# Attention over channels on one core: turned keys split by transfers inside SBUF, and the key sums' scale moved from the folded matrix to the queries

## The reference, cut to what matters

```
x = x + _L0_xattn_ref(_layernorm(x, axis=-1), ctx, Wq, Wkv, Wout, b_out, g)

q = einsum('oc,bcn->bon', Wq, x);  k, v = split(einsum('oc,bcn->bon', Wkv, context))
q = softmax(q over the 64 channels of a head) * 64 ** -0.5     # 8 heads of 64
k = softmax(k over the 1024 positions)
ctx = einsum('bhdn,bhen->bhde', k, v)
out = einsum('bhde,bhdn->bhen', ctx, q)
out = Wout @ out + b_out, then normalised over the 128 channels, times g
```

## Times and profile before

| | |
|---|---|
| time, median of 3 runs | 2017.39 us (2016.75 to 2019.11) |
| the profiled execution's own time | 2018.59 us |
| its span, first to last instruction | 2016.8 us |
| PE busy in the span | 1910.8 us (95%) |
| DVE busy | 1430.0 us (71%) |
| ACT busy | 996.2 us (49%) |
| POOL busy | 803.7 us (40%) |
| mean granted TensorE clock | 0.992 of full speed |

### The profile page before, as it was taken

The page is one execution under the profiler, slowest core; times in us unless marked ns, Lnnn a source line. Parts: engine busy times, 40 slices in busy tenths (PEclk is TensorE's granted clock), DMA queues, the critical chain, the costliest instruction groups (busy, mean ns, idle before and its releaser), DMA issues. The chain is left out here.

```text
span 2016.8 us, 29785 instructions
## 1 busy us (share of the span) xinstructions
PE 1910.8 (95%) x10780; PEld 1667.0 (83%) x10780; DVE 1430.0 (71%) x2049; ACT 996.2 (49%) x1207; POOL 803.7 (40%) x456
## 2 busy tenths in 40 slices
PE   4999999999999999999998789999999999999999
PEld 3778787878787878787877679999999999999998
DVE  5999999999999999999996664444444544444443
ACT  3777777777777777777776521111111111111111
POOL 3767676767676767676765000000000000000000
PEclk9999999999999999999999889999999999999999
DMA  3111111111111111111111621111111111111110
GB/s 116 47 67 59 68 56 67 59 67 56 68 60 67 58 66 60 66 58 66 60 35 47 179 93 56 49 53 62 62 62 62 62 62 62 62 57 48 51 42 32
DMA packets 43999, 127.64 MB, mean 63 GB/s; under 512 B 4224, under 2 KB 14080, under 8 KB 43968
## 3 DMA queue, kind: packets, MB, share of 16 engines
q1 hardware_dynamic: 39360, 110.44, 15.6%
q0 software_dynamic: 4608, 16.78, 2.6%
HBM read 93.65 MB, written 33.55 MB: 63 GB/s over the span
## 5 line engine op out<-in xcount | busy, mean ns | idle before, releaser
L281 POOL TENSOR_TENSOR kT_lo<-kT,kT_hi 128x1024 fp32r<-128x1024 f32 x128 | 304.7, 2403 | 0.6 <-ACT kT_hi L323 0.5
L277 POOL TENSOR_TENSOR eq<-eq,q_inv 128x1024 f32<-128x1024 f32 x128 | 242.5, 1905 | 143.8 <-DVE q_inv L487 143.8
L960 POOL TENSOR_TENSOR rstd_c<-var_c,minus_half 128x8 f32<-128x8 f32 x32 | 52.7, 1648 | 549.7 <-DVE var_c L1099 549.7
L52 PE MATMUL ps<-w_ra_hi,xT_hi 128*128 128x384 f32 (+1 forms) x768 | 257.2, 335 | 0.0
L54 PE MATMUL ps<-w_ra_hi,xT_lo 128*128 128x384 f32 (+1 forms) x768 | 251.7, 328 | 0.0
L53 PE MATMUL ps<-w_ra_lo,xT_hi 128*128 128x384 f32 (+1 forms) x768 | 251.4, 327 | 0.0
L982 ACT CAST hT_hi<-ps 128x512 fp32r<-128x512 f32 x64 | 37.7, 589 | 374.8 <-PE ps L1156 374.8
L52 PE MATMUL ps<-w_b_hi,hT_hi 128*128 128x512 f32 x512 | 205.4, 401 | 0.0
L338 ACT ACTIVATE ek<-ps,k_min 128x1024 f32<-128x1024 f32 x128 | 143.0, 1117 | 120.3 <-DVE k_min L491 120.3
L54 PE MATMUL ps<-w_b_hi,hT_lo 128*128 128x512 f32 x512 | 200.8, 392 | 0.0
L53 PE MATMUL ps<-w_b_lo,hT_hi 128*128 128x512 f32 x512 | 200.3, 391 | 0.0
(11 more groups left out here) (142 smaller groups left out, 4675.8 us busy)
## 6 DMA issues: line engine op xcount, KB each, us to landing
x_sb<-in_x SPq DMA_DIRECT2D x64, 512.0 KB, 4.1
ctx_sb<-in_ctx SPq DMA_DIRECT2D x32, 512.0 KB, 3.4
ctx_hi<-in_ctx POOLq DMA_DIRECT2D x32, 512.0 KB, 3.6
attention_out<-o_sb SPq DMA_DIRECT2D x32, 512.0 KB, 2.6
o_sb<-attention_out SPq DMA_DIRECT2D x32, 512.0 KB, 3.9
out<-out_sb SPq DMA_DIRECT2D x32, 512.0 KB, 2.9
x<-in_L_ffn_A SPq DMA_DIRECT2D x2, 512.0 KB, 4.1
o_sb<-in_L_ffn_A SPq DMA_DIRECT2D x2, 512.0 KB, 3.6
```

The source lines that it names most:

```text
L52: pe.matmul(out, stat_hi, mov_hi, start=first, stop=False)
L277: pool.tensor_tensor(v, v, per_row(q_inv[:, i, :], 2 * HEADS, DH), ALU.mult).then_inc(q_normed, 1)
L281: pool.tensor_tensor(kT_lo[:, i % 2, :, :], kT[:, i % 2, :, :], kT_hi[:, i % 2, :, :].bitcast(F32), ALU.subtract).then_inc(kT_lo_ready, 1)
```

## The change

Two things change in `attention`.

First, the key sums. `scale_m` and `m_full` go. The factor 64 ** -0.5 moves into Z's two parts, which are made once. One over the key sums is computed early in the step (`invert_keys`, a reciprocal into a double buffer) and multiplied into the turned queries while they are split: `query_hi` becomes an activation with a per-partition scale, `query_lo` a multiply-and-subtract. M is split straight out of PSUM: two casts of 64 x 512 on ACT and two subtractions of 64 x 512 on DVE, the slot being released by the last of these. ACT takes `folded_hi` ahead of `query_hi` 1. `shift_x` moves from DVE to ACT as two 128 x 1 activations.

Second, the turned keys. ACT still copies each piece from PSUM to `kT`. A transfer started by POOL copies `kT` to `kT_hi` in SBUF and converts on the way. ACT writes the negated, rounded `kT` into `kT_lo`, and a second transfer started by POOL adds `kT` to it. Both transfers count on one semaphore per piece, `kT_moved[i]`, for which PE and the copy of piece i+2 wait.

```diff
-        slot_read = {"K": k_exp, "C": cT_lo_ready, "Q": q_shifted, "KT": kT_copied, "M": m_scaled,
+        slot_read = {"K": k_exp, "C": cT_lo_ready, "Q": q_shifted, "KT": kT_copied, "M": m_lo_ready,
...
             def keys_lo(b, i):
-                pool.wait_ge(kT_hi_ready, 4 * b + i + 1)
-                pool.tensor_tensor(kT_lo[:, i % 2, :, :], kT[:, i % 2, :, :], kT_hi[:, i % 2, :, :].bitcast(F32),
-                                   ALU.subtract).then_inc(kT_lo_ready, 1)
+                pool.wait_ge(kT_copied, 4 * b + i + 1)
+                wait_for(pool, t_part, 4 * b + i - 1)
+                pool.sem_inc(kT_issued, 1)
+                pool.dma_start(kT_hi[:, i % 2, :, :], kT[:, i % 2, :, :]).then_inc(kT_moved[i], 16)
+                pool.wait_ge(kT_neg_ready, 4 * b + i + 1)
+                pool.sem_inc(kT_issued, 1)
+                pool.dma_start(kT_lo[:, i % 2, :, :], kT[:, i % 2, :, :], accum_op=ALU.add).then_inc(kT_moved[i], 16)
...
             def keys_copy(b, i):
                 act.wait_ge(kT_turned, 4 * b + i + 1)
-                wait_for(act, kT_lo_ready, 4 * b + i - 1)
+                if i >= 2:
+                    act.wait_ge(kT_moved[i - 2], 32 * b + 32)
+                else:
+                    wait_for(act, kT_moved[i + 2], 32 * b)
                 act.copy(kT[:, i % 2, :, :], slot(f"KT{i}")).then_inc(kT_copied, 1)
 
-            def keys_hi(b, i):
+            def keys_neg(b, i):
                 act.wait_ge(kT_copied, 4 * b + i + 1)
                 wait_for(act, t_part, 4 * b + i - 1)
-                act.copy(kT_hi[:, i % 2, :, :], kT[:, i % 2, :, :]).then_inc(kT_hi_ready, 1)
+                act.activation(kT_lo[:, i % 2, :, :], kT[:, i % 2, :, :], ACT.Copy, bias=0.0,
+                               scale=-1.0).then_inc(kT_neg_ready, 1)
...
-                act.copy(q_hi[:, j % 2, :], flat(f"QT{j}")).then_inc(q_hi_ready, 1)
+                act.activation(q_hi[:, j % 2, :], flat(f"QT{j}"), ACT.Copy, bias=0.0,
+                               scale=k_inv[:, p, j:j + 1]).then_inc(q_hi_ready, 1)
...
             def folded_hi(b):
-                act.wait_ge(m_scaled, 2 * b + 2)
+                act.wait_ge(m_made, b + 1)
                 wait_for(act, o_part, 4 * b)
-                act.copy(m_hi[:, :, :], m_full[:, :, :]).then_inc(m_hi_ready, 1)
+                for h in range(2):
+                    r = slice(h * DH, (h + 1) * DH)
+                    act.copy(m_hi[r, :, :], folded[r, :, h, :]).then_inc(m_hi_ready, 1)
...
-            def scale_m(b, p):
+            def invert_keys(b, p):
                 dve.wait_ge(k_exp, 4 * b + 4)
-                dve.reciprocal(k_inv[:, :], k_sum[:, p, :]).then_inc(k_inv_ready, 1)
-                dve.wait_ge(k_inv_ready, b + 1)
-                dve.wait_ge(m_made, b + 1)
-                wait_for(dve, m_lo_ready, b)
-                made = flat("M0").rearrange("p (j h c) -> p j h c", j=CH, h=2)
-                for h in range(2):
-                    r = slice(h * DH, (h + 1) * DH)
-                    dve.scalar_tensor_tensor(out=m_full[r, :, :], in0=made[r, :, h, :], scalar=DH ** -0.5,
-                                             in1=per_row(k_inv[r, :], CH, P), op0=ALU.mult,
-                                             op1=ALU.mult).then_inc(m_scaled, 1)
+                wait_for(dve, q_lo_ready, 4 * (b - 1))
+                dve.reciprocal(k_inv[:, p, :], k_sum[:, p, :]).then_inc(k_inv_ready, 1)
...
             def folded_lo(b):
-                dve.wait_ge(m_hi_ready, b + 1)
-                dve.tensor_tensor(m_lo[:, :, :], m_full[:, :, :], m_hi[:, :, :].bitcast(F32),
-                                  ALU.subtract).then_inc(m_lo_ready, 1)
+                for h in range(2):
+                    r = slice(h * DH, (h + 1) * DH)
+                    dve.wait_ge(m_hi_ready, 2 * b + h + 1)
+                    dve.tensor_tensor(m_lo[r, :, :], folded[r, :, h, :], m_hi[r, :, :].bitcast(F32),
+                                      ALU.subtract).then_inc(m_lo_ready, 1)
...
             def add_weighted(b, i):
-                pe.wait_ge(kT_lo_ready, 4 * b + i + 1)
+                pe.wait_ge(kT_moved[i], 32 * b + 32)
```

More of the change, by code:

```diff
@@ L109, in attention @@
         t_lo = sb("t_lo", [P, HD], F32R)
-        m_full = sb("m_full", [P, CH, P])
         m_hi = sb("m_hi", [P, CH, P], F32R)
@@ L114, in attention @@
         k_sum = sb("k_sum", [P, 2, CH])
-        k_inv = sb("k_inv", [P, CH])
+        k_inv = sb("k_inv", [P, 2, CH])
         q_max = sb("q_max", [P, 4, 2 * HEADS])
@@ L122, in attention @@
         rstd = sb("rstd", [P, 1])
+        neg_mean = sb("neg_mean", [P, 1])
         shift = sb("shift", [P, 1])
@@ L150, in attention @@
         q_lo_ready, cT_lo_ready = sem("q_lo_ready"), sem("cT_lo_ready")
[L151 to L154, removed]
+        t_lo_ready, k_inv_ready, m_lo_ready = sem("t_lo_ready"), sem("k_inv_ready"), sem("m_lo_ready")
+        x_stats, x_mean_ready, veps_ready = sem("x_stats"), sem("x_mean_ready"), sem("veps_ready")
         k_exp, q_exp, q_hi_ready = sem("k_exp"), sem("q_exp"), sem("q_hi_ready")
-        kT_copied, kT_hi_ready = sem("kT_copied"), sem("kT_hi_ready")
+        kT_copied, kT_neg_ready = sem("kT_copied"), sem("kT_neg_ready")
         cT_hi_ready, t_hi_ready, m_hi_ready, o_copied = (
             sem("cT_hi_ready"), sem("t_hi_ready"), sem("m_hi_ready"), sem("o_copied"))
+        neg_mean_ready, shift_ready = sem("neg_mean_ready"), sem("shift_ready")
         xn_ready, xn_hi_ready = sem("xn_ready"), sem("xn_hi_ready")
-        kT_lo_ready, q_normed = sem("kT_lo_ready"), sem("q_normed")
+        kT_issued = sem("kT_issued")
+        kT_moved, q_normed = [sem(f"kT_moved{i}") for i in range(CH)], sem("q_normed")
         ctx_hi_loaded = [sem(f"ctx_hi_loaded{i}") for i in range(2)]
@@ L178, in attention @@
         acc_flat = acc.rearrange("p a b -> p (a b)")
+        folded = flat("M0").rearrange("p (j h c) -> p j h c", j=CH, h=2)
         def on(kind, s, edge):
@@ L356, in folded_hi @@
             def folded_hi(b):
-                act.wait_ge(m_scaled, 2 * b + 2)
+                act.wait_ge(m_made, b + 1)
                 wait_for(act, o_part, 4 * b)
-                act.copy(m_hi[:, :, :], m_full[:, :, :]).then_inc(m_hi_ready, 1)
+                for h in range(2):
+                    r = slice(h * DH, (h + 1) * DH)
+                    act.copy(m_hi[r, :, :], folded[r, :, h, :]).then_inc(m_hi_ready, 1)
             def norm_x(b, p):
+                act.wait_ge(x_mean_ready, b + 1)
+                act.activation(neg_mean[:, :], mv[:, 0:1], ACT.Copy, bias=0.0, scale=-1.0).then_inc(neg_mean_ready, 1)
+                act.wait_ge(rstd_ready, b + 1)
+                act.wait_ge(neg_mean_ready, b + 1)
+                act.activation(shift[:, :], rstd[:, :], ACT.Copy, bias=0.0, scale=neg_mean[:, 0:1]).then_inc(shift_ready, 1)
                 act.wait_ge(shift_ready, b + 1)
@@ L381, in step @@
                     act.wait_ge(z_folded, 1)
-                    act.copy(z_hi[:, :], z_sum).then_inc(z_hi_ready, 1)
+                    act.activation(z_hi[:, :], z_sum, ACT.Copy, bias=0.0, scale=DH ** -0.5).then_inc(z_hi_ready, 1)
                 if KT:
                     keys_copy(s - 1, 0)
-                    keys_hi(s - 1, 0)
+                    keys_neg(s - 1, 0)
                     keys_copy(s - 1, 1)
-                    keys_hi(s - 1, 1)
+                    keys_neg(s - 1, 1)
                 if O:
@@ L395, in step @@
                     keys_copy(s - 1, 2)
-                    keys_hi(s - 1, 2)
+                    keys_neg(s - 1, 2)
                     keys_copy(s - 1, 3)
-                    keys_hi(s - 1, 3)
+                    keys_neg(s - 1, 3)
                 if K:
@@ L401, in step @@
                 if QT:
-                    query_hi(s - 1, 0)
+                    query_hi(s - 1, 1 - par, 0)
                 if Q:
@@ L408, in step @@
                     exp_keys(s, par, 2)
-                if QT:
-                    query_hi(s - 1, 1)
                 if M:
                     folded_hi(s - 1)
+                if QT:
+                    query_hi(s - 1, 1 - par, 1)
                 if Q:
@@ L415, in step @@
                 if QT:
-                    query_hi(s - 1, 2)
+                    query_hi(s - 1, 1 - par, 2)
                 if X_:
@@ L420, in step @@
                 if QT:
-                    query_hi(s - 1, 3)
+                    query_hi(s - 1, 1 - par, 3)
                 if K:
@@ L459, in weights, with query_lo @@
                 dve.tensor_tensor(w["bias"][:, :], b_col[:, :], b_mean[:, :], ALU.subtract).then_inc(b_step, 1)
-            def query_lo(b, j):
+            def query_lo(b, p, j):
                 dve.wait_ge(q_hi_ready, 4 * b + j + 1)
-                dve.tensor_tensor(q_lo[:, j % 2, :], flat(f"QT{j}"), q_hi[:, j % 2, :].bitcast(F32),
-                                  ALU.subtract).then_inc(q_lo_ready, 1)
```

(29 more changed lines are left out.)

9 lines of the change are left out of this document (3 added, 6 removed).

## The result

The changed kernel takes 2272.54 us (median of 4 runs, 2269.53 to 2275.02) against 2017.07 beside it: a ratio of 1.126, interval [1.1245, 1.1284]. The profiled execution took 2269.53 us with a span of 2267.9. Slower was forecast, but the forecast was 2111 us, +93 us, and the measured loss is +255. That is outside the forecast's own range (2028 to 2180) and where the rival "the accumulation costs two transfers or more" had put it (2208 to 2290).

The account below looks back on a forecast made before the run. PE was taken to set the pace at 33.64 us a step; the first part brought 32.4, transfer waits of 4.1 made 36.5, which over 32 batches is +93 us on 2018.6, so 2111 us, with its range from 2028 to 2180.

Parts of the forecast that it names:

- the accumulation costs two transfers or more: Rival on the keys' low-part transfers: 2208 us, up to 2290 with the store's collision and slower issue; chance 0.25.
- Lying between, with three passes for two, I take 2.25 and keep both ends: Data time of a 512 KB accumulating transfer: 2.25 us taken, between 1.5 (as a plain one) and 3.0.
- The prediction's own walk: Timing of four transfer pairs through POOL's queue: PE waits 1.4, 1.6 and 1.1 us at weighted 0, 1, 3; 4.1 per step.
- the second wait: PE's wait at weighted 1 for low part 1, seen at t = 13.4 but wanted at 11.8: 1.6 us.
- The 0.5 us before turn queries 2: New PE wait because M's slot is released by the second subtraction: about 0.5 us per step, bounds 0 and 0.8.
- The wait at the step's start: PE's wait for the exponentials of keys 3, some 0.2 us really lost, claimed to go as DVE gets lighter.
- cheap end: Accumulating transfer with 1.5 us of data: waits 0.7, 0.8 and 0, a step of 33.9 us, 2028 us.
- the store's collision: Output store's 1.4 us of data falls into low 0, adding up to that to the first wait: 2250 at the upper end.
- at 5 us or so behind its issue the forecast holds: Sign in the `kT_lo` landing: about 5 us the forecast, under 3.5 for low 0 the fast side, over 7 the dear case.
- the dear case: Accumulating transfers costing two plain ones or more: 2208 us, up to 2290; chance 0.25.
- The transfers are hidden: Rival: data time 1.2 us or less, or pairs overlap; waits 0.5, 0.2, 0, 2002 us, 1981 without waits; chance 0.22.
- The M chain gives nothing: Rival: M's slot released 1.5 us late, the first part's gain gone, +35 us; chance 0.05 with middling transfers (2146).

Follow-up runs that it names:

- high part on ACT: Changed kernel with the keys' high part cast by ACT, leaving POOL only the accumulating transfers: 2143.72 us, ratio 1.061 to the kernel before.
- half-size run: Changed kernel with each accumulating transfer cut to the first half of its bytes (256 KB), the other half's low part left out: 2117.39 us, ratio 1.048.
- waits filled: Changed kernel with throwaway products on TensorE ahead of weighted 0, 1 and 3 (9, 6 and 9): 2257.25 us, ratio 1.118.

## Why the prediction was wrong

The direction and the mechanism held: waits at weighted 0, 1 and 3, none at 2, the strict order on POOL, and the queue on the DMA engines. The size did not. Of the 161 us between 2111 and 2272, about 70 are the dearer accumulation, 20 the first part, 55 the store and the clock, and 17 are open.

- **The step that failed** is "Lying between, with three passes for two, I take 2.25 and keep both ends". An accumulating transfer has 2.8 us of data time (high part on ACT) where a plain one has 1.5. The half-size run shows that it is data time. The prediction's own walk at 3.0 us gave 2208, 97 us more than at 2.25. At 2.8 its waits are 2.0, 2.1 and 2.2, and it lies at about 2180. The issues were not the reason: an accumulating one lasts 0.87 us instead of 0.62, but in a row they start 0.57 to 0.59 apart.
- **The store and the clock.** The store was worked out at up to 1.4 us, used for the upper end only and left out of the sum. It cost 1.3 us. The fall of TensorE's clock behind a 2 us wait was put at nothing, without a word. It is also why the second wait looks right: 1.18 us against 1.6 is luck, since weighted 1 came 3.0 us later and the slow products of weighted 0 (2.7 us for its six instead of 1.5) filled 1.3 of these. Together they are 55 us (2272 to 2217), and neither shows its size alone.
- **The first part** was put at 38 us and gives 18. The 0.5 us before turn queries 2 was right (0.4). The wait at the step's start didn't go, and keys 3 got a new one.
- **What is open.** 2180 with 20 for the first part and 55 for store and clock gives 2255. The remaining 17 us, 0.5 us per step, weren't separated. Low 0 lands 0.9 us later than in the walk, at t = 10.5. The dearer data are 0.55 of it, and the norms, which end at t = 4.64 instead of 4.3, are the rest.
- **The walk at its cheap end.** The run with the second transfer plain has the 1.5 us that the walk took there for 2028. With 20 for the first part that is 2048, and it measured 2095, at a granted clock of 1.00. So the walk is too low even with the right data time and no fall of the clock. The 47 us are near what the prediction gave the store's collision (1.4 us x 32 = 45), but no run holds the store back there.
- **The sign** was misjudged. The landing of `kT_lo` read 5.3 us, which by "at 5 us or so behind its issue the forecast holds" was the forecast, and the time was the dear case's. By the walk itself low 0 lands 4.7 us behind its issue with 2.25 us of data, 5.3 with 2.8 and 5.5 with 3.0, so a landing time of some 5 us could not tell the cases apart. The other signs held: no wait at output 0, `m_lo` in two of 0.69, and POOL down to 19.1 us a step (forecast about 18).
- **The rule** of the Trainium skill (DMA: Bandwidth & Descriptors, "Anatomy of one DMA": 2.0 us and the bytes at 436 GB/s, an estimate of 3.2 us) fits a plain transfer inside SBUF. The run with the second transfer plain has 3.1 us for the high part, the first of its pair. It doesn't fit the accumulating one, 4.6 us with no transfer of its pair ahead of it. The prediction made 2008 of it in one place and 2002 in another from the same landings, and both are far off.
- **The other rivals.** "The transfers are hidden" is refuted even for two plain transfers (+94 us). "The M chain gives nothing" is refuted by the first part alone.

## What to carry to other kernels

A subtraction replaced by an accumulating transfer takes work off an engine that had room and puts 2.8 us of data per 512 KB on the DMA engines, where these transfers queue. Before moving work to the DMA engines, add up the data time of all that must land between two points of the bounding engine, other transfers included: here four pairs and a store (4 x 4.3 + 1.4 = 18.6 us) had to fit where the bound allowed some 12 (from the end of the norms, t = 4.6, to weighted 3, which stood at t = 16.8 before). When a fix yields less than the trace says it should, look at what took its place, and try it together with the other fix: two edits worth 11 and 15 us alone gave 55 together here.

## What the runs showed of the hardware that I had not expected

- An accumulating transfer of 512 KB inside SBUF lands 4.6 us after issue when the other of its pair is gone, and keeps the DMA engines busy for an estimated 2.8. A plain one beside it in the queue lands after 3.1 us (2.9 at least, in the changed kernel) and has 1.5. An issue of the first lasts 0.87 us on POOL, also at 256 KB, and of the second 0.58.
- A store of another queue, issued among such transfers, landed after 7.5 us instead of 2.6. Held back until they were through, it landed in 2.6 again.
- TensorE's granted clock fell to its lower level (1.2 GHz) for some 3.6 us about once per step (26 times in the 22 steps from 100 to 1000 us). TensorE had idled 1.7 to 2.8 us for a transfer before each fall, but other waits of 2.1 us had none behind them, and it was not always at the same one. With the waits filled the mean over these 900 us was 1.00.
- `m_lo` (128 x 512, both inputs in SBUF) took 1.82 us, with POOL subtracting in SBUF for the first 1.3 of them. Split in two of 64 x 512 that read one input from PSUM it took 1.41 in all. Which of the two differences made it shorter wasn't separated.
